# Loads of the shared weights split in two, an own home for the first context tile, and another order around the first step of attention

## What is computed

```python
x = x + tanh(g_xattn[0]) * retention(layernorm(x), ctx, ...)
x = x + tanh(g_ffn[0]) * moe(layernorm(x), ...)        # 8 experts, top 2, and a shared MLP of width 512
x = x + tanh(g_xattn[1]) * attention(layernorm(x), ctx, ...)
x = x + tanh(g_ffn[1]) * dense_moe(layernorm(x), ...)

# moe: routed + shared
h = gelu(einsum('nd,edh->neh', xf, w1) + b1);  routed = gates applied to einsum('neh,ehd->ned', h, w2) + b2
shared = gelu(xf @ shared_w1 + shared_b1) @ shared_w2 + shared_b2
# attention, 16 heads in 8 groups, width 128 each:
ln_out = ln(hidden)                       # divided by an input scale, clamped, rounded to fp8: one such row for q, qx, k, v
q, qx = ln(fp8_linear(ln_out, wq)), ln(fp8_linear(ln_out, wqx));  k = ln(fp8_linear(ln_out, wk));  v = fp8_linear(ln_out, wv)
kx, vx = split(ctx @ w_kv_x.T);  kx = ln(kx)
out = fp8_linear(concat(gqa(q, k, v), gqa(qx, kx, vx)), wproj)
```

## Time and profile before

| | us |
|---|---|
| median of the runs | 1801.33 |
| profiled execution, its own time | 1806.92 |
| its span | 1805.2 |
| PE busy | 1665.1 |
| ACT busy | 1107.8 |
| DVE busy | 1087.9 |
| POOL busy | 484.9 |

### The profile page before, as it was taken

How to read it: one execution, slowest core, us unless ns; L and a number is a source line. 1 busy time by engine, 2 the same in 40 slices (tenths; PEclk the granted TensorE clock), 3 DMA queues, 4 the chain that set the end, 5 groups by cost and what they waited for, 6 DMA issues and landing times. The chain is left out here.

```text
span 1805.2 us, 27250 instructions
## 1 busy us (share of the span) xinstructions
PE 1665.1 (92%) x9136; PEld 1363.7 (76%) x9136; DVE 1087.9 (60%) x2111; ACT 1107.8 (61%) x2975; POOL 484.9 (27%) x517
## 2 busy tenths in 40 slices
PE   6999659998995899999999999999999999966999
PEld 5888546666764778888888888788888788845887
DVE  6267564443874477777677776666665666666333
ACT  3353225553544887888888888877788877753000
POOL 1000022322423333333333333333333333301000
PEclk9999779999997999999999999999999999986999
DMA  6020637975563124246343263121161111010001
GB/s 241 34 70 1 266 123 263 315 249 195 190 247 134 47 70 165 99 158 257 123 169 111 99 234 125 53 99 48 40 239 54 53 52 39 32 76 1 24 29 41
DMA packets 74816, 219.61 MB, mean 122 GB/s; under 512 B 6288, under 2 KB 14480, under 8 KB 68304
## 3 DMA queue, kind: packets, MB, share of 16 engines
q1 hardware_dynamic: 69024, 199.56, 30.1%
q0 software_dynamic: 5680, 18.62, 3.4%
HBM read 157.60 MB, written 60.56 MB: 121 GB/s over the span
## 5 line engine op out<-in xcount | busy, mean ns | idle before, releaser
L2297 DVE TENSOR_TENSOR t_hn<-bank,t_rs 128x256 f32<-128x256 f32 (+1 forms) x256 | 130.9, 552 | 152.0 <-POOL t_rs L2016 75.5
L2042 PE MATMUL bank<-t_slot,t_x_q 128*128 128x512 f32 x512 | 205.8, 402 | 0.0
L2043 PE MATMUL bank<-t_slot,t_x_q 128*128 128x512 f32 x512 | 200.2, 391 | 0.0
L2013 POOL TENSOR_SCALAR t_ve<-t_ss 128x4 f32<-128x4 f32 (+1 forms) x128 | 25.2, 197 | 641.4 <-DVE t_ss L2293 620.5
L2216 ACT ACTIVATE t_sc<-bank,t_mx 128x128 f32<-128x128 f32 x512 | 183.8, 455 | 0.9 <-DVE t_mx L2317 0.9
L2016 POOL TENSOR_TENSOR t_rs<-t_ve,t_mhalf 128x4 f32<-128x4 f32 (+1 forms) x128 | 171.1, 1337 | 10.7
L2216 ACT ACTIVATION_READ_ACCUMULATOR t_sc<-bank,t_mx 128x1 f32 x512 | 151.3, 296 | 0.0
L2248 ACT ACTIVATE t_y<-bank,smooth 128x128 bf16<-128x128 f32 x512 | 139.1, 398 | 2.1 <-PE bank L2120 2.1
L2102 PE MATMUL bank<-t_hT 128*128 128x128 f32 x1024 | 131.1, 281 | 1.6 <-ACT t_hT L2237 1.6
L2102 PEld LDWEIGHTS bank<-t_hT 128*128 128x128 f32 x1024 | 120.1, 191 | 16.3 <-ACT t_hT L2237 15.8
L2324 DVE RECIPROCAL t_ri<-t_sm 128x4 f32<-128x4 f32 x128 | 22.7, 177 | 172.2 <-ACT t_sc L2216 172.2
(11 more groups left out here) (332 smaller groups left out, 4224.7 us busy)
## 6 DMA issues: line engine op xcount, KB each, us to landing
t_xh<-xq_scratch SPq DMA_DIRECT2D x64, 512.0 KB, 3.6
t_slot<-w_ready SPq DMA_DIRECT2D x16, 2048.0 KB, 8.5
t_cr<-in_ctxT_dram SPq DMA_DIRECT2D x64, 256.0 KB, 2.7
y_rows<-s_y SPq DMA_DIRECT2D x39, 256.0 KB
e_w<-in_w_units_dram SPq DMA_DIRECT2D x8, 1024.0 KB, 12.6
w_rows<-in_w_qkv_dram SPq DMA_DIRECT2D x8, 1024.0 KB, 6.9
w_ready<-w_hi SPq DMA_DIRECT2D x8, 1024.0 KB, 5.0
w_ready<-w_lo SPq DMA_DIRECT2D x8, 1024.0 KB
```

What stands on the lines that cost most here:

```text
L2042: nc.tensor.matmul(out, x_in[:, k, :], w[0][:, k, a:b], start=k == 0, stop=False)
L2043: last = nc.tensor.matmul(out, x_in[:, k, :], w[1][:, k, a:b], start=False, stop=k == KT - 1)
L2297: nc.vector.tensor_tensor(hn[:, lo:hi, :], b3[bk][:, 0:hi - lo, :], rs[:, lo:hi].unsqueeze(2).broadcast_to([P, hi - lo, P]), ALU.mult).the ...
```

## The change

`load_shared` takes a unit and is called twice: unit 0 after slot 30's store, once the even low stores have landed; unit 1 after slot 34's store, once the odd ones have. ACT waits for all high stores before it writes unit 0's high part. The first context tile gets three homes of its own (`cr0`, `c0_hi`, `c0_lo`, in the room of the hidden part), is loaded before the last weight load and split by POOL ahead of the second norm; tile 1 takes its place in both orders, and the wait for PE before the split begins with tile 2. The last scaled rows of chunk 2 go ahead of `squares_a(0)` on ACT, and their rounding goes behind `copy_last` on DVE.

```diff
-    def load_shared(self, sp, ready):
-        ready.all_stored(sp)
-        sp.dma_start(self.raw[0][:], self.env.dram["w_units"][E]).then_inc(self.raw_in0, 16)
-        sp.dma_start(self.raw[1][:], self.env.dram["w_units"][E + 1]).then_inc(self.raw_in1, 16)
+    def load_shared(self, sp, ready, u):
+        sp.wait_ge(ready.lo_st[u], 16 * (ready.count // 2))
+        sp.dma_start(self.raw[u][:], self.env.dram["w_units"][E + u]).then_inc((self.raw_in0, self.raw_in1)[u], 16)
...
             if s == SLOTS_N - 3:
+                act.wait_ge(self.ready.hi_st, 16 * self.ready.count)
                 self.units.hi_part(act, 0)
...
-            if s == 4 * ready.count + 1:
-                self.units.load_shared(sp, ready)
+            if s == 4 * ready.count - 2:
+                self.units.load_shared(sp, ready, 0)
+            if s == 4 * ready.count + 2:
+                self.units.load_shared(sp, ready, 1)
...
-        for j in range(J):
-            self.rounded(dve, C - 2, j)
+        for k in range(KT - 1):
+            self.rounded(dve, C - 2, k)
...
+    cr0 = sb("cr0", 112, [P, KT, P])
+    c0_hi = sb("c0_hi", 114, [P, KT, P], F32R)
+    c0_lo = sb("c0_lo", 116, [P, KT, P], F32R)
...
         def context(m):                                  # sync
+            if m == 0:
+                sp.wait_ge(sh.lo_in, C * sh.FS)
+            elif m == 1:
+                sp.wait_ge(sh.y_ps, C * J)
             if m:
                 sp.wait_ge(clo_in, m)
-            else:
-                sp.wait_ge(sh.y_ps, C * J)
-            sp.dma_start(cr[:], env.dram["ctxT"][m % B]).then_inc(cr_in, 16)
+            sp.dma_start((cr if m else cr0)[:], env.dram["ctxT"][m % B]).then_inc(cr_in, 16)
...
         weights(0, WQX, qx_w)
+        context(0)
         sp.wait_ge(sh.comb, 4 * C * 2)
         weights(0, KVX, kvx_w)
-        context(0)
+        context(1)
         x_rows(1)
         for k in range(KT):
             sh.store(sp, 2 * KT + k)
         wproj_rows(0)
-        context(1)
...
-            if later(m, 1):                              # gpsimd, context(m)
+            if later(m, 2):
                 pool.wait_ge(a_ps, m * 2)
...
+        pool.wait_ge(cr_in, 16)
+        nc.gpsimd.tensor_scalar(c0_hi[:], cr0[:], 1.0, None, ALU.mult).then_inc(chi_in, 1)
+        pool.wait_ge(chi_in, 1)
+        nc.gpsimd.tensor_tensor(c0_lo[:], cr0[:], c0_hi[:].bitcast(FP32), ALU.subtract).then_inc(clo_in, 1)
         pool.wait_ge(sh.y_ps, C * J)
         nc.gpsimd.memset(mhalf[:], -0.5).then_inc(half_in, 1)
         pool.wait_ge(half_in, 1)
         sh.second_norm(pool, C - 1)
-        context(0)
+        context(1)
         rstd(0, 0)
-        context(1)
         steps(pool, step)
...
+            hi, lo = (c_hi, c_lo) if later(m, 1) else (c0_hi, c0_lo)      # tensor
...
         sh.scaled(act, C - 2, 2)
+        sh.scaled(act, C - 2, 3)
         squares_a(0)
-        sh.scaled(act, C - 2, 3)
...
         sh.copy_last(dve)
+        sh.rounded(dve, C - 2, KT - 1)
         steps(dve, step)
```

More of the change, by code:

```diff
@@ L2064, in context_keys_values @@
                 pe.wait_ge(n_in, m * 4 - 2)
+            hi, lo = (c_hi, c_lo) if later(m, 1) else (c0_hi, c0_lo)
             for k in range(KT):
-                last = three_products(nc, bank[3][:], c_hi[:, k, :], c_lo[:, k, :], w[0][:, k, :], w[1][:, k, :],
-                                      k == 0, k == KT - 1)
+                last = three_products(nc, bank[3][:], hi[:, k, :], lo[:, k, :], w[0][:, k, :], w[1][:, k, :], k == 0,
+                                      k == KT - 1)
             last.then_inc(a_ps, 1)
```

## The result

The changed kernel took a median of 1786.1 us (1782.17 to 1790.27, six runs) beside 1800.92 us for the kernel before in six runs (1797.3 to 1801.56). The ratio is 0.9923 (95% interval 0.9905 to 0.9941): 13.9 us faster, 10.6 to 17.1. A second set gave 1786.69 beside 1801.32, ratio 0.9922 (0.9904 to 0.9939). The forecast was 1784 in 1777 to 1794, a gain of 17.4: the median lies in the range, 2.1 us over the forecast, and the forecast gain lies just above the interval.

A forecast was written before the change was run, and what follows sets the result against it. PE bounds the kernel, busy 92% of the span, so only waits before the loop's steady steps can go. 6.0 (slots' end) + 11.4 (opening) = 17.4 us off the median 1801.3 gives 1784, range 1777 to 1794.

The forecast's parts named there:

- The slots' end: End of the expert slots: slot 34's store no longer behind shared loads, so the first shared group starts 6.0 us earlier.
- That load: Unit 0's shared load beside a slot's gather, after slot 30's store: cost taken as 0, bounds 0 to 1.2 us.
- The opening: Opening of attention: the early context tile and new row order bring step 1's keys 11.4 us earlier, bounds 9 to 13.
- the 9.9 us between rounding and tile: Opening: from the last rounding's end to POOL's start on tile 2, behind the projection weights, taken unchanged at 9.9 us.
- the prediction's sign: Sign to look for in the profile after: the exponentials of step 1 come 17.4 us earlier.
- The rule of the page: Shared port lock of VectorE and GpSimd: tile 1's split ends 1.9 us later, first rstd 1.1, total gain 16.3 us.
- A: As a rival (0.20): half rate, port waits and x rows give back up to 4.4 us of the opening; time 1788.
- one of the prediction's signs of being wrong: Opening: x rows or tile 2 landing later than 12 us after the rounding would show the prediction wrong.
- B: As a rival (0.08): slot 34's store lands after 423 behind the last w_ready stores, losing the 6.0 us; time 1790.
- C: Rival (0.05): neither part works; tile 2 lands past 578 and slot 34's store is late; time 1801.
- D: As a rival (0.05): PE stays at half rate into the attention loop, 14 us more per step; slower, 1812.

The follow-up runs named there:

- e2: Kernel before with only the first context tile's own home and its order of loads and splits; rows and shared loads as before: 1790.1 us, ratio 0.9927.
- e4: Changed kernel with the two-step shared loads put back to one call at slot 33: 1792.65 us, ratio 0.9935.
- e3: Kernel before with only the row order changed: last scaled rows ahead of the first squares, their rounding behind the copies; 1803.02 us, ratio 1.0007.
- e7: Changed kernel with ACT's and DVE's row order as before, keeping two-step loads and the tile's home: 1784.25 us, ratio 0.9903.
- e5: Changed kernel with context tile 2 and x rows 2 loaded ahead of the last rows' store and the projection weights: 1786.34 us, ratio 0.9908.
- e9: Changed kernel with the edits of e5 and e8 together: 1785.63 us, ratio 0.992.
- e8: Changed kernel with POOL's first rstd ahead of its split of context tile 1: 1787.26 us in one run.
- e6: Changed kernel with context tile 2 and x rows 2 loaded ahead of the projection weights only, still behind the last rounding: 1783.18 us, ratio 0.9904.

## Why the prediction came out as it did

**The slots' end: the mechanism right, 6.0 forecast, 5.8 in the trace after, 4.5 on average, and 4.2 with what the first load costs ahead of it.** Every part is there: the store ahead of the second load, no wait of ACT, the high part at 416.98, the gap of 1.15 us, the last product in 1.98. From copy 34 to the first gelu of the shared part 21.57 us went by before and 15.80 after. Over all traces A is 30.34 on average with the old loads (before, e2 to e4) and 25.83 with the new ones (eight traces). Two things make up the difference. The trace on which the forecast rested had lost more than e2 and e3 (29.80 and 29.65; e4, like it, 30.89): its last product took 3.78 us, in e2 2.79. And two of the eight traces (e7 and e5) lost 4.2 and 1.8 us to the gather of the last slot's rows, which averages 0.7. That gather stood beside the last w_ready stores, which stand there in the kernel before too, and had landed before the second unit's load was issued (e7: 413.9 and 414.22; e5: 413.42 and 413.48). So it isn't shown that these waits belong to the change. They may: in both traces the store was issued 0.02 to 0.05 us behind the gather, in nine others 0.31 (in the changed kernel's first trace it was 0.76 ahead), and both had first waited 0.9 us for slot 36's gather, the one beside the first unit's load.

That load is the one for which the prediction gave 0 to 1.2 us and took 0, and its price lies ahead of A. PE stood idle before slot 36's rows for 0.56 to 1.68 us in five of the eight traces, and for 0.24 in all four with the old loads, which is its usual gap there. From the copy of slot 31 to that of slot 34 it took 12.31 us in those four and 12.31 to 13.39 in the eight, 0.3 more on average (the 0.9 us of e9 stand at slot 35). Single long waits for a gather aren't new: in the kernel before PE waited 3.13 us at 394.04, and in e8 a wait of 3.65 us, with the half rate behind it, made one slot take 8.85 us for 4.10. I can't say from these runs what decides which gather is late.

**The opening: 11.4 forecast; 10.9 measured at the keys of step 1, 11.1 at the first exponential, and 9.6 to 9.9 there where the turn is at half rate.** The steps one by one, in us into the opening, forecast (its times less 538.66) and then after: context product 0 ends 8.5, 8.5; normalised rows start 8.3, 8.26; keys of step 0 at 12.3, 13.53; copies done 15.6 to 16.4, 16.7; rounding done 18.1, 18.73; POOL starts tile 2 at 28.0, 28.57; keys of step 1 at 32.3, 32.86. The chain of causes held to the end, the 9.9 us between rounding and tile too (9.84). What the sum lacked is 1.2 us on DVE: the normalised rows beside POOL's split. It was partly returned, because the turn ran at full rate in that execution. From slot 34's copy to the first exponential it is 15.7 us less (155.90 for 171.59), where the prediction's sign said 17.4.

**The rule of the page.** The rows: the four normalised rows took 3.13 us beside the split and 1.92 with POOL idle (e8). POOL's split took 1.62 + 1.31 us there and 1.50 + 1.28 with DVE idle (tile 2 at 558.71), so it was stretched too, by 0.15; the 1.61 of before was itself beside a rounding. The Trainium skill (SBUF — State Buffer, "SBUF: two separate sides") gives the shared port pair, where VectorE's instruction needs it, to whichever of the two starts first, and has the other wait for the whole of it. The trace agrees in who is held up: POOL's split began at 537.33, DVE's rounding instruction at 537.34, and DVE's was the one stretched. It doesn't agree in how long: that instruction ended at 538.48, 0.5 us ahead of POOL's, where the rule would have held it until POOL's had ended. The prediction made POOL the loser, 1.9 us late, although the split starts first in its own times (545.85, and 547.0 for the normalised rows); DVE was stretched instead, by 1.2. So its gain by the rule, 16.3, came nearer than 17.4 by luck. Not every pair of instructions is hit: in e8 the split ran beside DVE's keys and its copies out of PSUM, and took 1.50 + 1.29 us, DVE's copies 0.68 us each as with POOL idle.

**Rivals.** A is partly true: half rate in the turn in some executions, and DVE's stretch. At the first exponential they leave 0.3 to 1.8 us less than the 11.4, not 4.4. The x rows of tile 2 cost nothing, though one of the prediction's signs of being wrong came true: they landed 12.1 us after the rounding's end (forecast 11.3, the sign 12), behind the 2 MB and tile 2. ACT converted them from 561.14 to 562.20, 0.8 us ahead of the keys at 563.00. B, C and D are refuted: store 34 was in time, tile 2 landed as forecast, and the loop's clock is 0.98 and then 1.00.

**What is left.** By the means of the traces the gain is 4.5 for A and 11.6 for D (137.82 without the tile's home; 126.25 in e4 and the two traces of the changed kernel), 16.1 together, less 0.3 ahead of A and 0.6 in B (95.90 on average in the nine traces with the tile's home, 95.28 in the three without). That makes 15.2, within the measured 10.6 to 17.1. Whether B's 0.6 belongs to the change is open. The first trace of the changed kernel, e8 and e9 have an added wait of 0.9 us for a low part, 28.4 us into B, behind a gather of the slots' outputs that POOL issued 1.1 us later than elsewhere; e4, e7 and e9 lose 0.4 to 0.9 us some 70 us into B, in e4 behind a store of rows. The changed kernel's second trace and e5 have neither, and all of it stands ahead of tile 0's load, 84 us into B. So no step of the prediction's chain failed. Its sum is 2.2 us too large by the traces, and 1.8 of that are in the first term, which was sized from one execution and took the gather beside the load at nothing.

**A part that gave nothing.** The prediction noted that every load behind the moved rounding waits for it, and left the sum of tile and order as it was. e2 and e3 show that the order alone returns nothing: without it the first exponential is 3.4 us earlier still. Its price in the time of the kernel isn't resolved, since the lead shrinks within the five steps behind (D of e7 123.16, of the changed kernel 124.35 and 127.29).

## What to carry to other kernels

A wait for a store can be an order in the DMA queue: look what SP issued ahead of it, and put a bulk load behind the store that somebody waits for. A mark reached earlier in a pipeline's filling is not yet time: in e5 6.2 us (7.6) won at the first exponential beside the changed kernel's first (second) trace were 1.7 (4.6) five steps later, since by then ACT waited for PE's queries. What is left there reaches the end. And size a stall from several executions where the trace shows waits that come and go; one profile shows the half rates and waits of its own run.

## What the runs showed of the hardware

- DVE's four 128x512 instructions on fp32 rows took 3.13 us beside POOL's split of a context tile and 1.92 beside an idle POOL; the int16 instruction of a rounding 1.14 and 0.69. POOL's split took 1.62 + 1.31 us there and 1.50 + 1.28 beside an idle DVE. Beside DVE's copies out of PSUM neither was stretched (e8).
- The same PE instructions behind the same idle time of 2.94 us ran at full rate in one execution (1.97 us) and at half rate in another of the same program (3.49 us).
- PE stood idle 0.2 to 2.1 us for the gather of most slots (4.3 us for the first), and 3.0 to 3.7 us at single ones, which were other slots in other executions of nearly the same program.
- A load of 256 KB on SP's queue landed 8.6 us after its issue behind a load of 2 MB, and 3.8 us after it with that load behind (e6).
